# One attention product moved ahead of the first v projection tile in the TensorE order of a two-layer graph attention kernel

## The reference

```
# layer 0: out = deg * (x Wi^T + b) + A (x Wj^T);  x = layernorm(x + out)
q, k, v = h @ Wq.T + bq, h @ Wk.T + bk, h @ Wv.T + bv      # 8 heads of 64
scores = (q @ k^T) / 8, masked where adj == 0
attn = softmax(scores);  out = (attn @ v) @ Wo.T + bo
x = layernorm(h + out)
```

## Time and profile before

| what | value |
|---|---|
| median of three runs | 2930.42 us (2930.1 to 2931.75) |
| the profiled execution's own time | 2929.39 us |
| its span | 2927.6 us |
| mean granted TensorE clock | 0.995 of full speed |
| PE busy | 2845.8 us, 97% of the span |
| DVE busy | 2257.1 us, 77% |
| POOL busy | 1883.1 us, 64% |
| ACT busy | 1871.3 us, 64% |
| DMA queue in use | 32.1% of 16 engines' span |

### The profile page before, as it was taken

How to read it: one execution, slowest core, us unless ns; L and a number is a source line. 1 busy time by engine, 2 the same in 40 slices (tenths; PEclk the granted TensorE clock), 3 DMA queues, 4 the chain that set the end, 5 groups by cost and what they waited for, 6 DMA issues and landing times.

```text
span 2927.6 us, 59805 instructions
## 1 busy us (share of the span) xinstructions
PE 2845.8 (97%) x18584; PEld 2456.9 (84%) x18584; DVE 2257.1 (77%) x5774; ACT 1871.3 (64%) x4874; POOL 1883.1 (64%) x1794
## 2 busy tenths in 40 slices
PE   6999999999999999999999999999999999999997
PEld 5888888888888888888888888888888888888886
DVE  7787777777877877777778778777787787777776
ACT  4666666666666666666666666666666666666665
POOL 5667666576676676665766766756657667666563
PEclk9999999999999999999999999999999999999999
DMA  4333333333333323333233333333332333333321
GB/s 137 109 101 102 114 102 106 107 101 111 103 100 115 100 100 115 100 107 107 97 111 107 100 112 103 100 111 104 107 106 97 113 107 101 110 105 101 107 95 57
DMA packets 282404, 306.71 MB, mean 105 GB/s; under 512 B 18816, under 2 KB 214912, under 8 KB 282368
## 3 DMA queue, kind: packets, MB, share of 16 engines
q1 hardware_dynamic: 282368, 306.26, 32.1%
HBM read 173.55 MB, written 132.64 MB: 105 GB/s over the span
## 4 chain that ended last, share of the span: by engine, by line
POOL 36%; issue 31%; PE 23%; DVE 7%; POOLq 1%; ACT 0%; DMA 0%; DVEq 0%; SPq 0%
PE proj L535 12%; POOL pT_lo L400 10%; POOL xb L395 5%; PE proj L498 4%; POOL probs L391 4%; POOL xs_lo L368 3%; PE attn L660 3%; DVE hb L1145 3%; POOL oT_lo L423 3%; POOL hb L409 2%; POOL mj_lo L379 2%; PE av L498 2%; POOL xs_raw L352 2%; POOL xs_raw L349 1%; DVE pT_lo L1078 1%
## 5 line engine op out<-in xcount | busy, mean ns | idle before, releaser
L400 POOL TENSOR_TENSOR pT_lo<-pT_raw,pT_hi 128x512 fp32r<-128x512 f32 x315 | 402.7, 1295 | 402.0 <-ACT pT_hi L856 402.0
L825 ACT ACTIVATE probs<-probs,row_min 128x256 f32<-128x256 f32 x1024 | 508.9, 499 | 225.5 <-DVE row_min L1043 222.2
L391 POOL TENSOR_TENSOR probs<-probs,row_inv 128x512 f32<-128x512 f32 x256 | 266.9, 1043 | 428.0 <-DVE row_inv L1054 428.0
L1043 DVE CUSTOM_DVE_ANT_0 probs<-attn,mask_add 128x256 f32<-128x256 f32 x1024 | 376.0, 419 | 43.3 <-PE attn L660 41.2
L862 ACT COPY o_part<-av 64x512 f32<-64x512 f32 x256 | 149.5, 584 | 393.5 <-PE av L498 388.9
L535 PE MATMUL proj<-wji_hi,xs_hi 128*128 128x512 f32 x896 | 363.2, 405 | 15.0 <-DVE wji_lo L1222 11.0
L535 PE MATMUL proj<-wji_lo,xs_hi 128*128 128x512 f32 x896 | 355.1, 396 | 0.0
L535 PE MATMUL proj<-wji_hi,xs_lo 128*128 128x512 f32 x896 | 355.1, 396 | 0.0
L1074 DVE STREAM_TRANSPOSE probs<-probs 128x1024 f32<-128x1024 f32 x189 | 234.8, 1242 | 113.9 <-PE av L498 113.9
L616 PE MATMUL proj<-mj_hi,wq_hi 128*128 128x256 f32 x1024 | 293.7, 287 | 11.3 <-DVE mj_lo L997 11.3
L1145 DVE TENSOR_SCALAR hb<-hb,mean_var_out,rstd_out 128x512 f32<-128x512 f32 x128 | 156.0, 1258 | 188.1 <-POOL rstd_out L418 188.1
(11 more groups left out here) (126 smaller groups left out, 8619.0 us busy)
## 6 DMA issues: line engine op xcount, KB each, us to landing
bounce<-probs SPq DMA_DIRECT2D x189, 512.0 KB, 2.6
pT_raw<-bounce SPq DMA_DIRECT2D x756, 128.0 KB, 3.0
xs_raw<-in_xT SPq DMA_DIRECT2D x64, 512.0 KB, 4.0
xb<-in_x SPq DMA_DIRECT2D x64, 512.0 KB, 3.4
out<-hb SPq DMA_DIRECT2D x64, 512.0 KB, 2.8
w_raw<-in_w0T SPq DMA_DIRECT2D x8, 256.0 KB, 5.8
stage<-in_wqT SPq DMA_DIRECT2D x1, 1024.0 KB, 10.1
stage<-in_wkT SPq DMA_DIRECT2D x1, 1024.0 KB, 12.0
```

Source lines behind the costliest of these rows:

```text
L391: pool.tensor_tensor(e, e, inv, ALU.mult).then_inc(norm_odd_done, 1)
L400: pool.tensor_tensor(pT_lo[:, g % 2, :, :, i, :, :], pT_raw[:, g % 2, :, :, i, :, :], pT_hi[:, :, :, i, :, :].bitcast(F32), ALU.subtract). ...
L825: last = nc.scalar.activation(e, e, ACT.Exp, bias=row_min[:, g % 2, s:s + 1], scale=-1.0, accum_out=row_sum[:, g % 2, s:s + 1])
L1043: last = V.tensor_tensor_reduce(out=out_, in0=in_, in1=mask_, scale=1.0, scalar=MIN_CEILING, op0=ALU.add, op1=ALU.min, accum_out=row_min[: ...
```

## The change

In the tensor engine's step, `attend(b, 2)` is issued before `v(n, 0)` and no longer after it. The same instructions are issued, with the same waits. The lists of the other engines, all semaphores' counts, buffers and DMAs are as before. The order of the last step and of the set-up, which do not use this list, is as before.

```
@@ -720,8 +720,8 @@
                 attend(b, 1)
                 k(n, 0)
                 k(n, 1)
+                attend(b, 2)
                 v(n, 0)
-                attend(b, 2)
                 v(n, 1)
                 attend(b, 3)
```

## The result

| | before | after |
|---|---|---|
| median | 2930.54 us | 3082.03 us (3074.22 to 3095.57) |
| ratio | 1 | 1.0521, 95% interval 1.0507 to 1.0536 |
| profiled execution, its span | 2929.39, 2927.6 us | 3095.57, 3093.8 us |
| mean granted TensorE clock | 0.995 | 0.964 |
| PE busy | 2845.8 us | 2926.8 us |

The change made the kernel 5.2% slower, 151 us, where 2985 us (+54) was forecast. The direction and the place of the loss were right. The size was not: the result lies outside the range given.

The account below looks back on a forecast made before the run. PE was taken to bound the kernel, busy 97%, with a recurring wait for DVE's low part. 39 x 1.64 less 22 x 0.43 is +54.5 us on 2929.39, median 1.0 above: 2985 us, range 2902 to 3031.

Parts of the forecast that it names:

- What bounds the kernel: PE, busy 97%; its last pair's product waits for DVE's low part (L1078), 26.1 us over 63 steps.
- The product can start early, with nothing waiting for it: On PE, pair 2's product starts 2.79 us earlier; its low parts are ready 1.06 us before, cost 0.
- Who goes next: Between DVE's two output-norm applies, a waiting POOL low part goes first, before DVE's second apply.
- The rival in which DVE keeps its turn: DVE's second apply goes first in every step: 61 x -0.43 = -26.2 us, 2904 us; 22 in 100.
- In how many steps: POOL goes first where pair 3's DMA lands in under 3.17 us: 39 steps, not the other 22.
- The price of a step with POOL first: DVE's second apply and low part are held up, so PE starts the last pair's product 1.64 us late.
- The other price that was weighed: Hand-overs from DVE to POOL 0.215 us dearer each: 2.07 us late or 0.21 gained per step, about 3006 us.
- The gain of a step with DVE first: POOL's low part follows DVE's second apply, and PE starts the last pair's product 0.43 us earlier.
- The sum: Whole kernel: 39 x 1.64 = 64.0, less 22 x 0.43 = 9.5, is +54.5 us.
- The forecast's own list of what would be seen: Signs: ACT's copy some 1.2 us after the first apply, longest second apply near 1.6, L1078 1.9, PE's wait about 80.

Follow-up runs that it names:

- the filled kernel: The changed kernel with eight 128x512 matmuls more in front of v's second tile in each step, their result overwritten: 3030.27 us, ratio 1.0339.
- the one with PE held back: The changed kernel, POOL's last-pair low part waiting for the first apply, PE's last-pair product waiting for POOL's long x_low: 3118.22 us, ratio 1.0638.
- both filled ones: Eight matmuls more before v's second tile: on the changed kernel, 3030.27 us; on the one with PE held back, 3043.73 us.

## Why the prediction was right or wrong

- **What bounds the kernel**: right. The wait for L1078 was the only one of PE that moved by more than 1.2 us with the change, and it moved the kernel both ways.
- **The product can start early, with nothing waiting for it**: right. ACT's copy is then bound by the landing of the DMAs, as its row says.
- **Who goes next**: right in kind. The waiting engine goes between two instructions of the other, also between two of the same kind with no wait between them. The rival in which DVE keeps its turn has fallen, except in the steps where POOL comes late.
- **In how many steps**: mis-sized, 39 forecast and 55 measured. "What decides is whether POOL's issue (landing + 0.74) comes before 1490.57" is 1.97 us after the first apply. In the changed kernel POOL was issued before that in 50 steps already, since the landings came out quicker (3.1 us or less in 48 steps, where the kernel before had 39). Five more went to POOL because it still goes first when it is issued up to 2.07 us after the first apply.
- **The price of a step with POOL first**: right, 1.64 us forecast and 46.41 - 44.77 = 1.64 measured with PE's gap filled; the two steps of the changed kernel without a fall of the clock show 1.55 and 1.60. The other price that was weighed, an estimate from the figure in the Trainium skill's "SBUF — State Buffer" ("A bandwidth-pool intuition that's wrong (but worth ruling out)"), would have made it 2.07; the page has it for GpSimd's writing of DMA descriptors. No run shows that price here: a waiting POOL instruction goes on as if from 0.1 us before DVE's recorded end.
- **The gain of a step with DVE first**: right, 0.43 forecast, 44.77 - 44.33 = 0.44 measured.
- **The sum**: here is the step that failed. The sum "39 x 1.64 = 64.0" takes PE's late start as the whole cost of a step with POOL first and puts what it does to PE's clock at nothing, without a reason. The late start leaves PE idle for 2 us, as the forecast itself had it ("a longest near 2.2"), and that costs clock worth 1.42 us more per step, nearly as much again. With the right count and no clock, the sum is 55 x 1.64 - 6 x 0.43 = +88 us; of the +166 us of the profiled execution the clock is the other 78. With 39 steps but with the clock, it would have been 39 x 3.06 - 9.5 = +110 us. The clock is the larger error; the number of steps is the smaller one.
- The forecast's own list of what would be seen held for three of four: copy 1.05 us after the apply (1.2 said), second apply 1.51 us (1.6), L1078 1.86 us (1.9). PE's wait was 110 us where 80 was said, for the number of steps.

The four executions of the changed kernel spread from 3074 to 3096 us, the one before by 2 us. It fits with a race for the turn that depends on DMA landings, step by step, but that isn't shown: only the profiled execution's steps were counted.

## What to carry to other kernels

A transfer or copy that is made earlier reaches its consumers in a new phase, and where two engines take turns on something, ask which gap of the one had been letting the other through. Before an early start is called free, lay the consumer's new issue time on the other engine's timeline; a wait that restores the old order (here one semaphore on POOL) can be worth more than the early start. And price a new idle stretch of PE twice: its length, and what the clock costs after it.

## What the runs showed of the hardware

- POOL and DVE take turns between single instructions, and a waiting one goes before the next of the other. What counts isn't the recorded issue: in the changed kernel POOL went first when issued up to 2.07 us after the first apply, 0.08 us after the recorded start of DVE's second apply, and came behind from 2.12 us on; in the filled kernel the two values are 2.02 and 2.09. The first apply ends at 2.05 to 2.08, and in the step with 2.07 it ends at 2.07. So the rows fit with a boundary at its end.
- Idle stretches of PE of 1.9 to 2.4 us, once a step, were followed by a granted clock of 0.50 for some 3 us in most steps (53 of 55 in the changed kernel, 53 of 61 in the one with PE held back); with 0.6 us or less at the same place (the kernel before, both filled ones) it fell in none of the 61 alike steps, and the mean clock stayed at 0.994 to 0.996.
- More matmuls made a kernel faster twice, by 52 us and by 74 us, with 504 of them added.
